# Node row and tile in one bf16 number: a placement product with 105 moving columns, and expert ids made last

## The chip, the cores and the metric

The kernel runs on one core of one Trainium2 chip. The metric is device time in microseconds (us), from the start of the program to its end. The engines named below are PE (TensorE matmul; its weight loads, PEld, are shown apart), DVE (VectorE), ACT (ScalarE), POOL (GpSimd) and SP (SyncE, which only issues DMAs here).

## What is computed

A graph layer for 6250 nodes with 256 features: a normalised graph convolution over 100,000 edges, a linear attention over all nodes, and a mixture of experts in which each node picks two of eight experts. The change touches only the step between the router and the experts:

```
logits = einsum('bsd,de->bse', xn, Wr) + br
top_vals, top_idx = top_k(logits, 2)
w = softmax(top_vals)
for e in range(8):
    h = gelu(xn @ W1[e] + b1[e])
    y = y + (h @ W2[e] + b2[e]) * w_full[..., e]
```

The kernel computes each expert only for the nodes that chose it. The 2 x 6250 choices are sorted by expert into 105 tiles of 128 slots, each tile of one expert. For each slot the kernel must know which node to gather and to which row of `results` its output is written.

## The kernel before

The program is a row of phases, each closed by a barrier over all engines (`over(phase)`). Two phases matter here: the router phase (about 834 to 1057 us) and the expert phase behind it (1058 to 1456 us).

**The place products.** At the end of the router phase, DVE knows for each of the 98 columns of choices (49 node tiles, two choices each) and each of the 128 rows the position of that choice in the sorted order, split into a tile number (`hi16`, 0 to 104) and a slot in the tile (`lo16`, 0 to 127). To invert this map the kernel uses PE. For each column c, `lo1` is the one-hot of the slot (128 x 128, the stationary operand) and `hv1` holds the one-hot of the tile times a value (the moving operand); the product adds that value at [slot, tile] of the PSUM bank `psI`. `hv1` has two halves of 105 columns: one with the one-hot times 2*row+1 (made by ACT, `own_rows`, L1498), one with the one-hot times the node's tile number (made by DVE, L1739). So 210 columns move in each of the 98 matmuls (L1458). bf16 holds a row value or a tile number exactly, but not their sum, which is why there are two halves.

The 98 columns go in `NROUND` = 7 rounds of `OHC` = 14. In a round DVE makes `hi1` (L1735), `lo1` (L1737) and the product `hv1` (L1739) for 14 columns in one instruction each; the 14 columns lie innermost in memory, so PE reads both operands with a step of 28 bytes from element to element. `hi1`, `lo1` and `hv1` are double buffered: DVE begins round r+2 when PE has ended round r (`pl_free`).

**Expert ids.** After round 0 DVE computes the expert of each of the 105 tiles (L1745 to L1749) and signals `eid_ok`. SP waits for it, between two parts of its list of stores, and loads the first two tiles' W1 (L1374, L1375).

**The normalised rows.** ACT makes 49 tiles of normalised rows (`norm`, L1495); SP stores them four tiles at a time in the DRAM array `table` (L1365, L1368), through a ring of four buffers (`keep`), from which the expert phase gathers. ACT does 34 of them, then the exponential of the router's softmax (L1510), then in each round two halves of `own_rows` and one `norm`, then the last eight.

**The end.** When the product is closed (L1461, a product with zeros), DVE reads `psI` and works out in eight instructions (L1756 to L1764) the gather index `gat` and the scatter index `sct` of every slot; slots without a node get a row behind the 12,500 real ones (`dump`). Then comes the barrier. In the expert phase POOL gathers rows (L1901), PE transposes them (L1813), multiplies with W1 (L1823) and W2 (L1833), and POOL scatters the result.

Of the kernel before, what the change touches and what calls it, by code (L numbers as in the profile page):

```python
# [4 lines left out]
f32, i32, bf16, f16 = mybir.dt.float32, mybir.dt.int32, mybir.dt.bfloat16, mybir.dt.float16  # L5
ALU, ACT, AX = mybir.AluOpType, mybir.ActivationFunctionType, mybir.AxisListType
P = 128

N, E, D = 6250, 100000, 256
NX, HID, EPS = 8, 512, 1e-5  # L10
# [3 lines left out]
T = -(-N // P)  # L14
# [37 lines left out]
def build(nc, a_x, a_src, a_dst, a_gw, a_cb, a_lnw, a_lnb, a_pre, a_wqkv, a_mk, a_mv, a_wout, a_bout,  # L52
# [5 lines left out]
    with ExitStack() as ctx:  # L58
# [1205 lines left out]
        def lanes(k):  # L1264
# [15 lines left out]
        held_i = rt[:, 1120:1120 + NTILE].bitcast(i32)  # L1280
# [7 lines left out]
        own_i, own = ints[:, 540:542], flat[:, 542:544]  # L1288
        tcol_i, tcol = ints[:, 550:550 + 2 * T], flat[:, 650:650 + T].bitcast(bf16)
# [7 lines left out]
        hv1 = [R2[:, 9408 + 1470 * k:9408 + 1470 * (k + 1)].bitcast(bf16).rearrange("p (j c) -> p j c", c=OHC)  # L1297
               for k in range(2)]
        w1r = RG[:, :].rearrange("p (s f) -> p s f", s=4)
# [9 lines left out]
        with nc.Block() as block:  # L1309
# [35 lines left out]
            pl_own = semaphore(phase, "r_place_rows")  # L1345
# [8 lines left out]
            @block.sync  # L1354
            def _(sp):
                sp.wait_ge(px_ok, T)
                sp.dma_start(R3[:, 0:room], a_w2).then_inc(w2_in, 16)
                sp.wait_ge(x_ok, T)
                sp.dma_start(b2s.rearrange("p e f -> p (e f)"), a_b2.unsqueeze(0).to_broadcast([P, NX * D])).then_inc(b2_in, 16)

                def keep_rows(h):
                    lo, n = 4 * h, min(4, T - 4 * h)
                    sp.wait_ge(n_ok, lo + n)
                    if lo + n < T:
                        sp.dma_start(table[lo * P:(lo + n) * P, :].rearrange("(t p) f -> p t f", p=P),  # L1365
                                     n_rows[:, 4 * (h % NR):4 * (h % NR) + n, :]).then_inc(keep[h % NR], 16)
                    else:
                        sp.dma_start(table[lo * P:N, :], n_rows[0:TAIL, 4 * (h % NR), :]).then_inc(keep[h % NR], 16)  # L1368

                for h in range(NB4 - 4):  # L1370
                    keep_rows(h)
                sp.wait_ge(eid_ok, 1)
                for t in range(2):
                    e = nc.sync.value_load(eid_i[0:1, t:t + 1], min_val=0, max_val=NX - 1)  # L1374
                    sp.dma_start(w1r[:, t, :], a_w1[bass.ds(e, 1), :, :].rearrange("a p f -> (a p) f")).then_inc(w_in[t], 16)  # L1375
                for h in range(NB4 - 4, NB4):
                    keep_rows(h)
                sp.wait_ge(w2_in, 16)
                for k in range(NR):
                    sp.wait_ge(keep[k], 16 * ((NB4 - k + NR - 1) // NR))  # L1380

            @block.tensor
            def _(pe):
# [69 lines left out]
                nc.tensor.matmul(psI[:, 0:2 * NTILE], zero16[:, 0:P], zero16[:, 0:2 * NTILE], start=True, stop=False)  # L1453
# [7 lines left out]
                nc.tensor.matmul(psI[:, 0:2 * NTILE], zero16[:, 0:P], zero16[:, 0:2 * NTILE], start=False,  # L1461
# [3 lines left out]
            def _(act):  # L1465
# [32 lines left out]
                def own_rows(r, k):  # L1498
                    if k == 0:
                        act.wait_ge(pl_hot, r + 1)  # L1500
                        if r >= 2:
                            act.wait_ge(pl_free, r - 1)
                    act.activation(hv1[r % 2][:, 0:NTILE, k:OHC:2], hi1[r % 2][:, :, k:OHC:2], ACT.Copy,
                                   scale=own[:, k:k + 1]).then_inc(pl_own, 1)

                early = 34
# [4 lines left out]
                act.wait_ge(ready, 3)  # L1511
                for r in range(NROUND):
                    for k in range(2):
                        own_rows(r, k)
                    norm(early + r)
                for t in range(early + NROUND, T):
                    norm(t)

            @block.gpsimd
            def _(pool):  # L1520
# [3 lines left out]
                nc.gpsimd.iota(own_i, pattern=[[1, 2]], base=1, channel_multiplier=2).then_inc(pl, 1)  # L1524
                nc.gpsimd.iota(dump_i, pattern=[[P, NTILE]], base=2 * N + 1, channel_multiplier=1).then_inc(pl, 1)
                nc.gpsimd.iota(tcol_i, pattern=[[1, T], [0, 2]], base=0, channel_multiplier=0).then_inc(pl, 1)
                pool.wait_ge(pl, 3)
                nc.gpsimd.tensor_copy(dump, dump_i).then_inc(pl, 1)
                nc.gpsimd.tensor_copy(own, own_i).then_inc(ready, 1)
                nc.gpsimd.tensor_copy(tcol, tcol_i).then_inc(ready, 1)  # L1530
# [10 lines left out]
            def _(v):  # L1541
# [188 lines left out]
                def place(r):  # L1730
                    if r >= 2:
# [7 lines left out]
                    nc.vector.tensor_tensor(hv1[r % 2][:, NTILE:2 * NTILE, :], hi1[r % 2],  # L1739
                                            tcol[:, here].unsqueeze(1).to_broadcast(wide), ALU.mult).then_inc(pl_tile, 1)  # L1740

                for r in range(NROUND):
                    place(r)
                    if r == 0:
                        ch.done(nc.vector.tensor_tensor(past, iwin[0:1, 0:NSTEP].unsqueeze(2).to_broadcast([1, NSTEP, NX - 1]),  # L1745
                                                        cumt[0:1, 0:NX - 1].unsqueeze(1)
                                                        .to_broadcast([1, NSTEP, NX - 1]), ALU.is_ge))
                        ch.done(nc.vector.tensor_reduce(eidf, past, AX.X, ALU.add))
                        nc.vector.tensor_copy(eid_i, eidf).then_inc(eid_ok, 1)  # L1749
# [266 lines left out]
```

## Time and profile before

| | us |
|---|---|
| median of 3 runs | 1534.99 (1532.45 to 1539.14) |
| profiled execution, its own time | 1534.88 |
| span of its instructions | 1532.9 |
| PE busy / weight load busy | 1266.2 / 1107.0 |
| DVE / ACT / POOL busy | 960.1 / 450.8 / 764.0 |
| mean granted TensorE clock | 0.934 |

Times in the trace count from the span's start. The page's L418 line is the same kind of product in the first phase, where the in-degrees are counted: 14 columns a round, both operands with the same 28-byte step, the stationary one 128 wide, the moving one 49. A timeline row gives the start, the length from first start to last end of a run of like instructions, the engine, the line, the operation and its count, and in brackets how long the engine had been idle and what ended that. The granted clock is a share of 2.4 GHz, so 0.50 is 1.2 GHz. A matmul's duration reaches from its start to the end that the profiler models, so back-to-back matmuls overlap; the distance of their starts tells the rate.

### The profile page before, as it was taken

To read this page: it belongs to the slowest core of one execution; us is meant where nothing else is said; L and a number is where in the kernel's file an instruction comes from. 1 tells how busy PE (TensorE), PEld (TensorE's weight loads), DVE (VectorE), ACT (ScalarE), POOL (GpSimd) and SP (SyncE) were. 2 spreads that over 40 slices of the span, in tenths; PEclk is the share of its full clock that TensorE was granted. 3 is DMA by queue.
4 is the path that set the end of the run, shared out by engine and by line. 5 is a ranking of instruction groups with operands and counts; after the bars stand their busy time and mean duration, and the time that the engine had idled before them with its cause. 6 is when DMAs were issued, how large, how long until landed. Compare 5 with 4: busy or idle time off the path is not lost. (4 is left out here: it accounts for less than half of the span.)

```text
span 1532.9 us, 30179 instructions
## 1 busy us (share of the span) xinstructions
PE 1266.2 (83%) x8310; PEld 1107.0 (72%) x8311; DVE 960.1 (63%) x2700; ACT 450.8 (29%) x1322; POOL 764.0 (50%) x822
## 2 busy tenths in 40 slices
PE   1797678888888999998987978767999999999910
PEld 1685477887787889887775856523999999999900
DVE  3998777777688888778854977863222223222347
ACT  1565600122123333333221023463322332233200
POOL 2001577777777777777774023201555555555400
PEclk9999898999999999999998989955999999999965
DMA  6002533333466667778895000252666666666658
GB/s 204 15 0 69 168 106 105 104 105 106 126 177 174 199 196 215 211 219 261 279 283 166 1 1 1 108 181 94 211 210 209 216 209 210 212 215 207 192 198 314
DMA packets 142678, 248.24 MB, mean 162 GB/s; under 512 B 22826, under 2 KB 99108, under 8 KB 142324
## 3 DMA queue, kind: packets, MB, share of 16 engines
q1 hardware_dynamic: 99256, 146.13, 29.8%
q0 software_dynamic: 34320, 93.76, 21.0%
q10 hardware_dynamic: 9004, 7.21, 1.4%
q8 instruction: 41, 0.67, 0.2%
q14 instruction: 57, 0.47, 0.1%
HBM read 213.65 MB, written 33.36 MB: 161 GB/s over the span
## 5 line engine op out<-in xcount | busy, mean ns | idle before, releaser
L716 POOL DMA_INDIRECT RG<-table,srci x504 | 496.0, 984 | 157.7 <-issue 154.4
L733 PE MATMUL ps<-S_t,RG 128*128 128x96 f32 x2016 | 283.7, 278 | 51.7 <-DMA RG<-table,srci 47.8
L733 PEld LDWEIGHTS ps<-S_t,RG 128*128 128x128 f32 x2016 | 270.3, 195 | 74.8 <-DMA RG<-table,srci 60.8
L1881 DVE TENSOR_TENSOR R<-ps,R 128x256 f32<-128x256 f32 x105 | 44.6, 425 | 278.4 <-PE ps L1833 278.4
L1823 PE MATMUL ps<-R,RG 128*128 128x128 f32 x1680 | 207.2, 277 | 0.0
L987 DVE TENSOR_TENSOR R<-R,ps 128x392 f32 x280 | 157.0, 561 | 79.3 <-PE ps L743 59.7
L755 PE MATMUL ps<-zrow,R 128*128 128x256 f32 x686 | 193.3, 386 | 12.8 <-DMA zrow<-table 7.9
L1856 ACT ACTIVATE R<-ps,RG 128x128 f32<-128x128 f32 x420 | 119.7, 368 | 279.0 <-PE ps L1823 279.0
L1833 PE MATMUL ps<-R 128*128 x840 | 198.6, 380 | 0.0
L1823 PEld LDWEIGHTS ps<-R,RG 128*128 128x128 f32 x1680 | 198.4, 194 | 0.0
L1907 POOL DMA_INDIRECT results<-R,S_t x105 | 103.7, 988 | 164.0 <-DVE R L1881 160.8
L1833 PEld LDWEIGHTS ps<-R 128*128 128x128 f32 x840 | 151.8, 191 | 16.1
L1901 POOL DMA_INDIRECT R<-table,S_t x105 | 101.9, 971 | 104.4 <-PEq L1806 71.6
L755 PEld LDWEIGHTS ps<-zrow,R 128*128 128x128 f32 x686 | 121.6, 190 | 33.1 <-DMA zrow<-table 16.4
L859 ACT ACTIVATE R<-iwin 128x256 f32<-128x256 f32 (+2 forms) x127 | 61.4, 490 | 174.1 <-PE ps L755 164.1
L418 PE MATMUL ps<-RG 128*128 128x49 bf16 x784 | 82.4, 276 | 15.1 <-DVE RG L509 15.1
L418 PEld LDWEIGHTS ps<-RG 128*128 128x128 bf16 x784 | 72.6, 144 | 25.0 <-DVE RG L509 21.5
L1534 POOL TENSOR_TENSOR R<-R,slot 128x256 f32<-128x256 f32 x49 | 35.6, 727 | 109.5 <-DVE slot L1618 109.4
L1872 DVE TENSOR_SCALAR R<-ps,gamma,beta 128x128 f32<-128x128 f32 x212 | 76.6, 403 | 11.9 <-PE ps L1813 11.9
L946 DVE TENSOR_TENSOR S_t<-dstrel,iwin 128x384 f32<-128x384 f32 x126 | 69.4, 551 | 0.7
L508 DVE TENSOR_TENSOR RG<-R,RG 128x1792 bf16<-128x1792 bf16 x56 | 61.0, 1090 | 8.4 <-PE ps L418 8.0
L959 DVE TENSOR_TENSOR R<-R,ps 128x192 f32 x126 | 44.4, 353 | 30.9 <-issue 27.9
(352 smaller groups left out, 1883.3 us busy)
## 6 DMA issues: line engine op xcount, KB each, us to landing
RG<-in_w SPq DMA_DIRECT2D x106, 514.0 KB
zrow<-table SPq DMA_DIRECT2D x336, 128.0 KB
R<-results SPq DMA_DIRECT2D x48, 256.0 KB, 12.2
RG<-table,srci POOLq DMA_INDIRECT x504, 3.4
table<-RG SPq DMA_DIRECT2D x12, 512.0 KB, 2.9
table<-R SPq DMA_DIRECT2D x12, 512.0 KB, 3.3
out<-R ACTq DMA_DIRECT2D x48, 128.0 KB, 5.4
R<-in_x SPq DMA_DIRECT2D x6, 896.0 KB
```

What stands on the lines that cost most here:

```text
L418: last = nc.tensor.matmul(ps[7][:, 0:T], ohlo[k][:, :, c], ohhi[k][:, :, c], start=False, stop=False)
L716: nc.gpsimd.indirect_dma_start(out=grows[:, s, :], out_offset=None, in_=table, in_offset=bass.IndirectOffsetOnAxis(ap=srci[:, ND + q, c:c ...
L733: last = nc.tensor.matmul(window(q % 2)[:, h, :], grows[:, s, h * P:(h + 1) * P], S_t[:, q % 2, c, :], start=c == 0, stop=c == GC - 1)
L755: nc.tensor.matmul(psD[:, 0:D], adj[b % 2][0:n, j, :], zrow[0:n, i % ZR, :], start=j == 0, stop=j == T - 1).then_inc(z_used, 1)
L946: nc.vector.tensor_tensor(S_t[:, q % 2, :, :], dstrel[:, ND + q, :].unsqueeze(2).to_broadcast([P, GC, WIN]), iwin[:, 0:WIN].unsqueeze(1).t ...
L987: nc.vector.tensor_tensor(win, win, psK[m % 2][:, 0:T * DW].rearrange("p (j w) -> p j w", w=DW), ALU.add).then_inc(cnt_ok, 1)
L1823: last = nc.tensor.matmul(psH[s % 2][:, h * P:(h + 1) * P], w1r[:, s, k * HID + h * P:k * HID + (h + 1) * P], ur[:, s % 2, k, :], start=k ...
L1833: last = nc.tensor.matmul(psY[s % 2][:, 0:D], hr[:, s % 2, h, :], w2_sb[:, bass.ds(e, 1), h, :].rearrange("p a f -> p (a f)"), start=h == ...
L1856: last = act.activation(hr[:, s % 2, h, :], psH[s % 2][:, h * P:(h + 1) * P], ACT.Gelu, bias=w1r[:, s, KC * HID + h:KC * HID + h + 1])
L1872: last = nc.vector.tensor_scalar(ur[:, s % 2, k, :], psX[s % 2][:, k * P:(k + 1) * P], gamma[:, k:k + 1], beta[:, k:k + 1], ALU.mult, ALU.add)
L1901: nc.gpsimd.indirect_dma_start(out=xr[:, t % 4, :], out_offset=None, in_=table, in_offset=bass.IndirectOffsetOnAxis(ap=gat[:, t:t + 1], ax ...
L1907: nc.gpsimd.indirect_dma_start(out=results, out_offset=bass.IndirectOffsetOnAxis(ap=sct[:, t:t + 1], axis=0), in_=yr[:, t % 4, :], in_offs ...
```

## The change

One bf16 number carries both values. For column j = 2*tile + choice and row p, an int16 is made with the bits 128*(134 + j) + p, and read as bf16: p stands in the seven bits of the significand, 134 + j in the exponent. A one-hot times this number is exact, and a sum with zeros in PSUM too. POOL makes the array `code` at the start of the phase (L1512, L1515 of the changed kernel). `hv1` is now 105 columns wide and made by DVE alone, ACT's `own_rows` and its semaphore are gone, and PE waits for DVE only. After the products DVE takes tile, choice and row out of the bits with shifts and masks: twelve instructions in place of eight.

The expert ids are computed after the last round instead of after round 0, and SP issues all thirteen stores of rows before it waits for them. ACT does 24 rows, the exponential, and then the other 25 rows without a break.

```
-        hv1 = [R2[:, 9408 + 1470 * k:9408 + 1470 * (k + 1)].bitcast(bf16).rearrange("p (j c) -> p j c", c=OHC)
+        hv1 = [R2[:, 9408 + 735 * k:9408 + 735 * (k + 1)].bitcast(bf16).rearrange("p (j c) -> p j c", c=OHC)
                for k in range(2)]
+        CODE0 = 134 * P
...
-                for h in range(NB4 - 4):
+                for h in range(NB4):
                     keep_rows(h)
                 sp.wait_ge(eid_ok, 1)
...
-                for h in range(NB4 - 4, NB4):
-                    keep_rows(h)
...
                     pe.wait_ge(pl_tile, r + 1)
-                    pe.wait_ge(pl_own, 2 * r + 2)
                     for c in range(OHC):
-                        last = nc.tensor.matmul(psI[:, 0:2 * NTILE], lo1[r % 2][:, :, c], hv1[r % 2][:, :, c],
+                        last = nc.tensor.matmul(psI[:, 0:NTILE], lo1[r % 2][:, :, c], hv1[r % 2][:, :, c],
...
-                early = 34
+                early = 24
...
-                act.wait_ge(ready, 3)
-                for r in range(NROUND):
-                    for k in range(2):
-                        own_rows(r, k)
-                    norm(early + r)
-                for t in range(early + NROUND, T):
+                for t in range(early, T):
                     norm(t)
...
+                nc.gpsimd.iota(code_i, pattern=[[P, 2 * T]], base=CODE0, channel_multiplier=1).then_inc(pl, 1)
+                nc.gpsimd.tensor_copy(code16, code_i).then_inc(ready, 1)
...
-                    nc.vector.tensor_tensor(hv1[r % 2][:, NTILE:2 * NTILE, :], hi1[r % 2],
-                                            tcol[:, here].unsqueeze(1).to_broadcast(wide), ALU.mult).then_inc(pl_tile, 1)
+                    nc.vector.tensor_tensor(hv1[r % 2], hi1[r % 2], code[:, here].unsqueeze(1).to_broadcast(wide),
+                                            ALU.mult).then_inc(pl_tile, 1)
...
                 ch.done(nc.vector.tensor_copy(held, psI[:, 0:NTILE]))
-                ch.done(nc.vector.scalar_tensor_tensor(held, psI[:, NTILE:2 * NTILE], float(2 * P), held, ALU.mult,
-                                                       ALU.add))
-                nc.vector.tensor_scalar(pad, held, 0.5, None, ALU.is_lt)
-                ch.done(nc.vector.tensor_scalar(held_i, held, -1.0, 0.0, ALU.add, ALU.max))
-                ch.done(nc.vector.tensor_scalar(gat, held_i, 1, None, ALU.arith_shift_right))
-                ch.done(nc.vector.tensor_tensor(pad, pad, dump, ALU.mult))
-                ch.done(nc.vector.scalar_tensor_tensor(pad, held, -1.0, pad, ALU.add, ALU.add))
-                ch.done(nc.vector.tensor_copy(sct, pad))
+                ch.done(nc.vector.tensor_scalar(code_q, held.bitcast(i32), 16, None, ALU.arith_shift_right))
+                nc.vector.tensor_scalar(tile_q, code_q, 8, None, ALU.arith_shift_right)
+                nc.vector.tensor_scalar(row_q, code_q, P - 1, None, ALU.bitwise_and)
+                ch.done(nc.vector.tensor_scalar(pad, held, 0.5, None, ALU.is_lt))
+                ch.done(nc.vector.tensor_scalar(tokf, tile_q, float(-(CODE0 >> 8)), float(P), ALU.add, ALU.mult))
+                nc.vector.tensor_tensor(pad, pad, dump, ALU.mult)
+                ch.done(nc.vector.tensor_tensor(tokf, tokf, row_q, ALU.add))
+                ch.done(nc.vector.tensor_scalar(gat, tokf, 0.0, None, ALU.max))
+                ch.done(nc.vector.tensor_scalar(code_q, code_q, 7, 1, ALU.arith_shift_right, ALU.bitwise_and))
+                ch.done(nc.vector.scalar_tensor_tensor(pad, gat, 2.0, pad, ALU.mult, ALU.add))
+                ch.done(nc.vector.tensor_tensor(sct, pad, code_q, ALU.add))
```

What stands in a row on DVE, at the first two rounds of the kernel before (L1745, L1748 and L1749 are the expert ids):

```order
L1735 TENSOR_TENSOR R2<-R3,RG 128x1470
L1737 TENSOR_TENSOR R2<-R3,RG 128x1792
L1739 TENSOR_TENSOR R2<-R2,S_t 128x1470
L1745 TENSOR_TENSOR slot<-iwin,R3 1x742
L1748 TENSOR_REDUCE R3<-slot 1x106
L1749 CAST S_t<-R3 1x106
L1735 TENSOR_TENSOR R2<-R3,RG 128x1470
```

And on DVE at the last round of the changed kernel (L1729, L1732 and L1733 are the expert ids there, L1735 to L1737 the softmax weights, L1740 the first read of `psI`):

```order
L1720 TENSOR_TENSOR R2<-R3,RG 128x1470
L1722 TENSOR_TENSOR R2<-R3,RG 128x1792
L1724 TENSOR_TENSOR R2<-R2,S_t 128x1470
L1729 TENSOR_TENSOR slot<-iwin,R3 1x742
L1732 TENSOR_REDUCE R3<-slot 1x106
L1733 CAST S_t<-R3 1x106
L1735 TENSOR_SCALAR x1s<-x1b 128x49
L1736 RECIPROCAL x1s<-x1s 128x49
L1737 TENSOR_TENSOR x1b<-x1b,x1s 128x49
L1740 COPY R3<-ps7 128x105
```

The three instructions of the expert ids moved from between rounds 0 and 1 to behind round 6.

On SP, the same place in the kernel before (`table` is written by the stores, `in_w1` read by the first two weight loads):

```order
L1365 DMA table<-R2 128x4x256 x9
L1374 TENSOR_LOAD S_t
L1374 ISA x2
L1375 ISA
L1375 DMA RG<-in_w1 128x1028
L1374 TENSOR_LOAD S_t
L1374 ISA x2
L1375 ISA
L1375 DMA RG<-in_w1 128x1028
L1365 DMA table<-R2 128x4x256 x3
L1368 DMA table<-R2 106x256
```

And in the changed kernel:

```order
L1368 DMA table<-R2 128x4x256 x12
L1371 DMA table<-R2 106x256
L1377 TENSOR_LOAD S_t
L1377 ISA x2
L1378 ISA
L1378 DMA RG<-in_w1 128x1028
L1377 TENSOR_LOAD S_t
L1377 ISA x2
L1378 ISA
L1378 DMA RG<-in_w1 128x1028
```

The two weight loads moved behind the last four stores.

## Rows read from the trace of the kernel before

**Rows 1.** Windows: us, busy (xcount) of PE PEld DVE ACT POOL, PEclk, DMA, GB/s
```profile
1007.00:1054.70 47.70, 37.89 (x100) 14.02 (x100) 26.52 (x42) 29.64 (x45) 0.00 (x0) 0.50 0.34 112
...
1065.00:1456.00 391.00, 390.44 (x2705) 364.29 (x2706) 112.07 (x312) 118.57 (x416) 199.76 (x204) 0.99 0.67 206
```

**Rows 2.** Timeline of PE, end of the router phase and first expert tiles
```profile
1017.16 37.36 PE L1458 MATMUL ps<-R 128*128 128x210 bf16 x98 [9.75 <-ACT R L1503]
1054.35 0.35 PE L1461 MATMUL ps<-slotb 128*128 128x210 bf16 x1
1063.25 0.69 PE L1813 MATMUL ps<-ident,R 128*128 128x128 f32 x2 [8.55 <-DMA R<-table,S_t]
...
1066.04 3.62 PE L1823 MATMUL ps<-R,RG 128*128 128x128 f32 x16
...
1074.37 1.84 PE L1823 MATMUL ps<-R,RG 128*128 128x128 f32 x15
```

**Rows 3.** Timeline of DVE over rounds 0 to 2
```profile
1012.06 0.93 DVE L1735 TENSOR_TENSOR R<-R,RG 128x1470 bf16<-128x1470 bf16 x1
...
1013.91 0.92 DVE L1739 TENSOR_TENSOR R<-R,S_t 128x1470 bf16<-128x1470 bf16 x1
1014.74 0.91 DVE L1745 TENSOR_TENSOR slot<-iwin,R 1x742 f32<-1x742 f32 x1
...
1016.77 0.91 DVE L1735 TENSOR_TENSOR R<-R,RG 128x1470 bf16<-128x1470 bf16 x1
...
1022.69 0.93 DVE L1735 TENSOR_TENSOR R<-R,RG 128x1470 bf16<-128x1470 bf16 x1 [3.18 <-PE ps L1458]
```

**Rows 4.** Instructions by line: duration ns min/median/max, first and last start
```profile
L1458 PE MATMUL ps<-R x98: 551/559/563, 1017.2 to 1054.0; 128*128 128x210 bf16 x98
...
L418 PEld LDWEIGHTS ps<-RG x784: 138/142/168, 44.3 to 134.5; 128*128 128x128 bf16 x196
...
L421 PE MATMUL ps<-slotb x1: 225/225/225, 134.7 to 134.7; 128*128 128x49 bf16 x1
```

**Rows 5.** Timeline of PE's weight loads, one round of the in-degree product
```profile
55.44 1.30 PEld L418 LDWEIGHTS ps<-RG 128*128 128x128 bf16 x14 [0.16 <-DVE RG L509]
```

**Rows 6.** Timeline of ACT from the second batch of norms on
```profile
1004.56 8.95 ACT L1495 ACTIVATE R<-R,zs_b,zs_s 128x256 f32<-128x256 f32 x18 [4.27 <-DMA table<-R]
1013.53 1.28 ACT L1510 ACT_TABLE_LOAD   x1
...
1014.97 2.05 ACT L1503 ACTIVATE R<-R,S_t 128x735 bf16<-128x735 bf16 x2
```

**Rows 7.** SP: two rows of its timeline, one of its waits (us, times, longest)
```profile
1021.46 1.84 SPq L1375 DMA_DIRECT2D RG<-in_w  x2
...
1051.40 0.33 SPq L1368 DMA_DIRECT2D table<-R  x1
...
SPq L1380 <- DMA table<-R: 4.8, 2, 4.6
```

**Rows 8.** Timeline of DVE from its last round to the end of the phase
```profile
1046.62 0.18 DVE L1751 TENSOR_SCALAR x1s<-x1b 128x49 f32<-128x49 f32 x1
...
1047.34 0.21 DVE L1753 TENSOR_TENSOR x1b<-x1b,x1s 128x49 f32<-128x49 f32 x1
1054.81 0.27 DVE L1756 COPY R<-ps 128x105 f32<-128x105 f32 x1 [7.26 <-PE ps L1461]
...
1055.41 0.22 DVE L1759 TENSOR_SCALAR R<-R 128x105 f32<-128x105 f32 x1
1055.54 0.21 DVE L1760 TENSOR_SCALAR R<-R 128x105 int32<-128x105 f32 x1
1055.79 0.22 DVE L1761 TENSOR_SCALAR S_t<-R 128x105 int32<-128x105 int32 x1
1056.04 0.27 DVE L1762 TENSOR_TENSOR R<-R,S_t 128x105 f32<-128x105 f32 x1
...
1056.65 0.22 DVE L1764 CAST S_t<-R 128x105 int32<-128x105 f32 x1
```

More of the change, by code:

```diff
@@ L5 @@
 f32, i32, bf16, f16 = mybir.dt.float32, mybir.dt.int32, mybir.dt.bfloat16, mybir.dt.float16
+i16 = mybir.dt.int16
 ALU, ACT, AX = mybir.AluOpType, mybir.ActivationFunctionType, mybir.AxisListType
@@ L1279, in build @@
         held = rt[:, 1010:1010 + NTILE]
-        held_i = rt[:, 1120:1120 + NTILE].bitcast(i32)
+        code_q = rt[:, 1120:1120 + NTILE].bitcast(i32)
+        tokf = rt[:, 1240:1240 + NTILE]
+        tile_q, row_q = (rt[:, 610 + 110 * k:610 + 110 * k + NTILE].bitcast(i32) for k in range(2))
         tl_i = rt[:, 1230:1230 + NX].bitcast(i32)
@@ L1287, in build @@
         dump_i = ints[:, 430:430 + NTILE]
-        own_i, own = ints[:, 540:542], flat[:, 542:544]
-        tcol_i, tcol = ints[:, 550:550 + 2 * T], flat[:, 650:650 + T].bitcast(bf16)
+        code_i, code16 = ints[:, 550:550 + 2 * T], flat[:, 650:650 + T].bitcast(i16)
+        code = flat[:, 650:650 + T].bitcast(bf16)
         hi1 = [R2[:, 735 * k:735 * (k + 1)].bitcast(bf16).rearrange("p (j c) -> p j c", c=OHC) for k in range(2)]
@@ L1344, in build @@
             pl_tile = semaphore(phase, "r_place_tiles")
-            pl_own = semaphore(phase, "r_place_rows")
             pl_free = semaphore(phase, "r_place_used")
@@ L1452, in _ @@
                 pe.wait_ge(cum_ok, 1)
-                nc.tensor.matmul(psI[:, 0:2 * NTILE], zero16[:, 0:P], zero16[:, 0:2 * NTILE], start=True, stop=False)
+                nc.tensor.matmul(psI[:, 0:NTILE], zero16[:, 0:P], zero16[:, 0:NTILE], start=True, stop=False)
                 for r in range(NROUND):
                     pe.wait_ge(pl_tile, r + 1)
-                    pe.wait_ge(pl_own, 2 * r + 2)
                     for c in range(OHC):
-                        last = nc.tensor.matmul(psI[:, 0:2 * NTILE], lo1[r % 2][:, :, c], hv1[r % 2][:, :, c],
+                        last = nc.tensor.matmul(psI[:, 0:NTILE], lo1[r % 2][:, :, c], hv1[r % 2][:, :, c],
                                                 start=False, stop=False)
                     last.then_inc(pl_free, 1)
-                nc.tensor.matmul(psI[:, 0:2 * NTILE], zero16[:, 0:P], zero16[:, 0:2 * NTILE], start=False,
+                nc.tensor.matmul(psI[:, 0:NTILE], zero16[:, 0:P], zero16[:, 0:NTILE], start=False,
                                  stop=True).then_inc(inv_ok, 1)
@@ L1496, in norm @@
                                    bias=zs_b[:, t:t + 1]).then_inc(n_ok, 1)
[L1498 to L1504, printed above, removed]
-                early = 34
+                early = 24
                 for t in range(early):
@@ L1523, in _ @@
                                allow_small_or_imprecise_dtypes=True).then_inc(ready, 1)
[L1524 to L1530, printed above, removed]
+                nc.gpsimd.iota(dump_i, pattern=[[P, NTILE]], base=2 * N, channel_multiplier=1).then_inc(pl, 1)
+                nc.gpsimd.iota(code_i, pattern=[[P, 2 * T]], base=CODE0, channel_multiplier=1).then_inc(pl, 1)
+                pool.wait_ge(pl, 2)
+                nc.gpsimd.tensor_copy(dump, dump_i).then_inc(ready, 1)
+                nc.gpsimd.tensor_copy(code16, code_i).then_inc(ready, 1)
                 def residual(t):
@@ L1738, in place @@
                     v.wait_ge(pl_hot, r + 1)
-                    nc.vector.tensor_tensor(hv1[r % 2][:, NTILE:2 * NTILE, :], hi1[r % 2],
-                                            tcol[:, here].unsqueeze(1).to_broadcast(wide), ALU.mult).then_inc(pl_tile, 1)
+                    nc.vector.tensor_tensor(hv1[r % 2], hi1[r % 2], code[:, here].unsqueeze(1).to_broadcast(wide),
+                                            ALU.mult).then_inc(pl_tile, 1)
                 for r in range(NROUND):
                     place(r)
[L1744 to L1749, printed above, removed]
+                ch.done(nc.vector.tensor_tensor(past, iwin[0:1, 0:NSTEP].unsqueeze(2).to_broadcast([1, NSTEP, NX - 1]),
+                                                cumt[0:1, 0:NX - 1].unsqueeze(1)
+                                                .to_broadcast([1, NSTEP, NX - 1]), ALU.is_ge))
+                ch.done(nc.vector.tensor_reduce(eidf, past, AX.X, ALU.add))
+                nc.vector.tensor_copy(eid_i, eidf).then_inc(eid_ok, 1)
                 v.wait_ge(ex_ok, 1)
```

## The prediction

> **What bounds the kernel now.** I read the stretches first, then the timelines of PE, DVE, ACT and SP over the 50 us before the expert phase. The expert phase is one stretch in which PE is busy 390.44 of 391 us at a granted clock of 0.99 [rows 1]; its length doesn't depend on when it starts, so whatever the router phase gives up moves the end of the program by the same amount. In the router phase the place product decides. From 1017.16 to 1054.70 PE does 98 matmuls without a pause [rows 2]; DVE, which feeds them, stands still for 3.18 us before round 2 until PE frees a buffer [rows 3], and for 7.26 us at the end until PE closes the product [rows 8]. After that come DVE's eight index instructions, to 1056.87, and 6.38 us of barrier, gather and first transpose, to 1063.25 [rows 2, 8]. SP's last store, issued by 1051.73, had landed after a wait of 4.6 us, at about 1056.3 [rows 7], so DVE closes the phase, with SP only 0.6 us ahead. The clock is 0.50 through the product, that is 1.2 GHz [rows 1].
>
> **PE's start.** The product starts at 1017.16, released by ACT [rows 2]. ACT was late: 34 norms, a table load and the exponential kept it until 1015, then it needed 2.05 us for the two halves of round 0 [rows 6]. DVE's own part of round 0 ended at 1013.91 + 0.92 = 1014.83 [rows 3]. With ACT out of it PE starts a semaphore later, 0.06 us: 1014.89, which is 2.27 us earlier.
>
> **PE's rate, the term that carries the sum.** The 98 matmuls take 37.36 us, of which the last one's own duration is 0.559 [rows 2, 4]: (37.36 - 0.559)/97 = 0.379 us from start to start, or 1.807 ns for each of 210 moving columns. The trace has no product with 105 such columns, but it has one with 49, same weight shape and same step in memory, L418. Fourteen of its weight loads take 1.30 us including the last one's 0.142 [rows 4, 5]: (1.30 - 0.142)/13 = 0.0891 us, or 1.818 ns a column. Both are proportional to the columns with nothing left for a fixed part, if both ran at the same clock. The profile gives 1.00 for that early stretch, but the closing matmul L421 with 49 packed columns took 0.225 us, and L1461 with 210 at 0.50 took 0.35 [rows 2, 4]: 0.125 to 0.13 us for 161 columns is 0.79 ns each, about one cycle at 1.2 GHz. A matmul at 2.4 GHz would not lie on that line. I take it that L418 ran at 1.2 GHz too and that the 1.00 stands only for "no change recorded yet". Then 105 columns take 105 x 1.807 = 0.190 us, and a round of 14 takes 2.66 us in place of 5.31. The upper bound, if L418 did run at full clock, comes from adding the 128 weight columns to the moving ones: 0.379 x 233/338 = 0.261 us, 3.66 us a round. I take 0.190, since it needs no coincidence.
>
> The rule of the Trainium skill that speaks of this (TensorE: Matmul & The Clock Gate, "Back-to-back issue gap") gives one cycle a column, 87.5 ns for 105 at 1.2 GHz, with 107 ns for the weights. The trace disagrees: 379 ns for 210 where the rule gives 175. By the rule the sum would be that of rival B below. The Trainium skill (SBUF — State Buffer), in the note on 16-byte cachelines under its port table, also says that reads whose step crosses such a line pay a penalty, and the step here is 28 bytes; the trace agrees.
>
> **DVE and PE together.** DVE's three instructions of a round keep it 2.68 us when nothing holds it (1012.06 to 1014.74) and are complete after 2.77 [rows 3]. Round r+2 needs the buffer of round r. After PE starts round r, DVE may begin r+2 after 13 x 0.190 + 0.37 + 0.05 = 2.89 us (0.37 is the duration 0.559 less 105 columns; 0.05 is 1022.69 less the end of PE's round 0). Then 2.77 to build and 0.06 to start PE: 5.72 us for two rounds, while PE itself needs 5.32 and DVE 5.36. So neither engine alone is the bound, but the hand-over through two buffers. PE starts rounds 0, 2, 4, 6 at 1014.89, 1020.61, 1026.33, 1032.05. The closing matmul starts at 1032.05 + 2.66 = 1034.71. DVE read PSUM 0.46 us after that point before [rows 2, 8]; with 0.09 less for 105 packed columns it reads at 1035.08. Before it was 1054.81: **19.73 us earlier**.
>
> **Expert ids made last.** They took 2.03 us after round 0 (1014.74 to 1016.77) [rows 3]. That was hidden, since DVE then waited 3.18. Now they stand behind round 6: DVE begins that round at 1026.33 + 2.89 = 1029.22, is free at 1031.90, has the ids at 1033.93 and the softmax weights 0.97 later (1046.62 to 1047.55 and the step on) [rows 8], at 1034.90. PE's last round covers it, with 0.18 us to spare. Cost 0; if PE were faster it would show, up to 3.0 us.
>
> **SP.** Its waiting instruction is now the one for the ids, with nothing behind it but the two weight loads; all stores are issued before. It issues the loads about 0.8 and 2.3 us after 1033.93 (two took 1.84 us from first to last [rows 7]), done at 1036.6. The phase ends for DVE at 1037.9, so it isn't held. The loads are needed when the first hidden product starts, 2.79 us behind the first transpose (1066.04 - 1063.25) [rows 2], now about 1047: 10 us later. The second load may still be moving when the first gather is; I allow 0 to 1 us, take 0.
>
> **ACT and the stores.** ACT waited 4.27 us for the ring after 16 norms and did 18 more in 8.95 us [rows 6], 0.50 each. Now it does 8, the exponential (1.5 us) and 25: 1004.56 + 4.0 + 1.5 + 12.5 = 1022.6. Stores follow and land by about 1027 even with the 4.6 us of the last one. That is 10 us before anyone needs them; cost 0. The removed `own_rows` were ACT's, the removed POOL instructions stood at the start of the phase ahead of nothing that waits.
>
> **The index instructions.** Before: 1054.81 to 1056.87, 2.06 us. Steps read there [rows 8]: an instruction that the next waits for costs its duration and 0.03 to 0.04, so 0.25 for a TENSOR_SCALAR and 0.30 for a copy from PSUM or a two-operand one; one without a wait costs 0.13 (1055.41 to 1055.54), a two-operand one then about 0.18. Now: one copy 0.30, five waited scalar steps (L1741, L1744, L1745, L1748, L1749) 1.25, two unwaited 0.26, one unwaited two-operand 0.18, two waited two-operand 0.60, the last 0.27: 2.86 us. **0.80 us more.** Shifts and masks on integers cost the same as others (L1761).
>
> **Sum.** -19.73 + 0.80 = -18.9 us. Against the profiled execution's 1534.88: 1516.0. That execution lies 0.1 us from the median of the runs, 1534.99, so the forecast is **1516.0 us**.
>
> **Rivals.**
> (A) PE's rate isn't proportional: 0.261 us a matmul. Then PE is the bound, seven rounds of 3.66 us from 1014.89, the closing matmul at 1040.5, DVE reads at 1040.9: 13.9 us earlier, less 0.8. 1521.8 us. For it speaks the 1.00 shown at L418; against it L421's duration.
> (B) PE is faster than I take it and DVE alone sets the pace: round 6 begins at 1014.74 + 5 x 2.68 = 1028.14, is done 2.68 later, and ids and softmax weights, 3.0 us, lie bare: read at 1033.8, 21.0 us earlier, less 0.8. 1514.7 us. It would also follow if the granted clock rose in the product. Against both stands a matmul stream that took 379 ns a matmul and stayed at 0.50 for 37 us [rows 1, 2]. The Trainium skill's one cycle a column (TensorE: Matmul & The Clock Gate, "Back-to-back issue gap") would give this case.
> (C) The change doesn't do what it says: the stream is bound by the strided weights, which stay 128 wide, at 0.379 us. Only the earlier start stays: 2.27 + 0.09 less 0.8. 1533.3 us. Against it: L418 loads the same weights every 0.089 us [rows 5].
> (D) Slower: the clock. PE enters the expert phase at 0.50 after a gap of 8.55 us, and 16 matmuls of L1823 take 3.62 us where later 15 take 1.84 [rows 2]. A tile costs 1.66 us more there, and the W2 half, with as many column passes, the same: 3.3 us. Before, the clock was full within three tiles. If the shorter product left PE at the low clock for more tiles, six of them eat the gain, and eight more make 1542 us. Against it: after 37 us of matmuls the clock was still 0.50, so the product bought nothing there, and the gap stays the same.
>
> **How the numbers follow.** Forecast, within 3 us of 1516: 0.66. Rival B 0.08, A 0.13, C 0.05, D 0.03. The rest, 0.05, is my sum with something between 3 and 6 us laid bare (the weight loads against the first gathers, a late store). All but C and D are faster by more than 0.5% (7.7 us, about what a measurement of this kernel can tell from no change): faster 0.91; same 0.06 (C and part of the rest); slower 0.03. The range takes in B with a little scatter of the runs and A: 1512 to 1522.5; it leaves out C, D and the end of the rest.
>
> **What would show it.** In the changed kernel: 98 matmuls of 128x105 in about 20 us, 0.190 from start to start, at 0.50; DVE starting rounds 2 to 6 on PE's release, with waits of a few tenths only; ids made under the last round; ACT idle after about 1023; two W1 loads issued at about 1035; the first read of `psI` at 1035.1 and the phase's last DVE instruction near 1037.9; the first gather 1.9 us later; the expert phase as long as before, its first two tiles at the low clock. Wrong would be: a distance of 0.26 or 0.38 between matmuls, PE waiting for the first W1, or a clock that stays at 0.50 past the third tile.

## The result and the profile after

The changed kernel took 1520.33 us, median of four runs (1520.58, 1520.08, 1514.08 and one run of 4200.72, for which the record shows no cause and which is left out of the comparison), against 1534.84 for the kernel before, also of four. The ratio of the others is 0.9891, 95% interval 0.9869 to 0.9913, so the kernel is faster by 0.9 to 1.3%, between 13 and 20 us. Forecast were 1516.0 us and a range of 1512 to 1522.5. The profiled execution took 1520.58 us (span 1518.8), 14.3 us less than the profiled one before.

The timeline of PE over the same place as [rows 2] (L1458 is the place product, L1461 closes it, L1800 is the first transpose of the expert phase, L1810 the W1 product; a row gives start, length, count and the idle time before):

```profile
1019.74 17.13 PE L1458 MATMUL ps<-R 128*128 128x105 bf16 x84 [7.55 <-DVE R L1724]
1037.02 2.90 PE L1458 MATMUL ps<-R 128*128 128x105 bf16 x14 [0.16 <-DVE R L1724]
1039.74 0.27 PE L1461 MATMUL ps<-slotb 128*128 128x105 bf16 x1
1049.22 0.69 PE L1800 MATMUL ps<-ident,R 128*128 128x128 f32 x2 [9.21 <-DMA R<-table,S_t]
...
1051.84 3.62 PE L1810 MATMUL ps<-R,RG 128*128 128x128 f32 x16
```

The product that took 37.36 us now takes 20.2. In its last round 14 matmuls take 2.90 us, of which 0.37 are the last one's own duration, so they start 0.195 us apart (forecast 0.190). The product is released by DVE (L1724, the multiplication that makes `hv1`), not by ACT. DVE over the same rounds as [rows 3] and up to the reading of `psI` as in [rows 8]:

```profile
1016.92 0.92 DVE L1720 TENSOR_TENSOR R<-R,RG 128x1470 bf16<-128x1470 bf16 x1
...
1018.76 0.92 DVE L1724 TENSOR_TENSOR R<-R,S_t 128x1470 bf16<-128x1470 bf16 x1
1019.60 0.92 DVE L1720 TENSOR_TENSOR R<-R,RG 128x1470 bf16<-128x1470 bf16 x1
...
1022.69 0.93 DVE L1720 TENSOR_TENSOR R<-R,RG 128x1470 bf16<-128x1470 bf16 x1 [0.34 <-PE ps L1458]
...
1028.44 0.93 DVE L1720 TENSOR_TENSOR R<-R,RG 128x1470 bf16<-128x1470 bf16 x1 [0.28 <-PE ps L1458]
...
1034.20 0.93 DVE L1720 TENSOR_TENSOR R<-R,RG 128x1470 bf16<-128x1470 bf16 x1 [0.29 <-PE ps L1458]
...
1036.88 0.91 DVE L1729 TENSOR_TENSOR slot<-iwin,R 1x742 f32<-1x742 f32 x1
...
1039.61 0.21 DVE L1737 TENSOR_TENSOR x1b<-x1b,x1s 128x49 f32<-128x49 f32 x1
1040.11 0.27 DVE L1740 COPY R<-ps 128x105 f32<-128x105 f32 x1 [0.30 <-PE ps L1461]
...
1042.70 0.27 DVE L1751 TENSOR_TENSOR S_t<-R 128x105 int32<-128x105 f32 x1
```

DVE's waits in the product have shrunk from 3.18 to about 0.3 us, one in every second round: that is the hand-over through two buffers. The expert ids (from L1729) and softmax weights (to L1737) lie under PE's last round, with 0.30 us to spare. ACT and SP, as in [rows 6] and [rows 7]:

```profile
1014.83 12.40 ACT L1495 ACTIVATE R<-R,zs_b,zs_s 128x256 f32<-128x256 f32 x25
...
1027.25 0.33 SPq L1371 DMA_DIRECT2D table<-R  x1
1039.92 1.52 SPq L1378 DMA_DIRECT2D RG<-in_w  x2
```

ACT is done at 1027.2 and the last store is issued by 1027.6, 15 us before DVE ends the phase; the two weight loads are issued by 1041.4, 1.5 us before DVE ends the phase.

All these times lie 4.86 us later than they should beside the kernel before: round 0 begins at 1016.92 in place of 1012.06, although little ahead of it was changed: instructions of POOL that nobody waits for, a narrower product with zeros that opens `psI`, and, in the last 4 us, the order of ACT's work. This offset is what separates 1520.6 from the forecast. Counted from round 0:

| from the start of round 0, us | before | after | difference | forecast |
|---|---|---|---|---|
| PE's first product | 5.10 | 2.82 | -2.28 | -2.27 |
| DVE reads `psI` | 42.75 | 23.19 | -19.56 | -19.73 |
| last index instruction ends | 44.81 | 26.05 | -18.76 | -18.93 |
| first W1 product | 53.98 | 34.92 | -19.06 | -18.9 |
| end of the span | 520.84 | 501.88 | -18.96 | -18.9 |

### The profile page after: what moved, and what is told of

Read it like the earlier page. It is cut to its first block and busy times, and to the rows that moved or that the text cites. A ratio compares the mean times of both kernels' runs of the same rounds, so it can differ in the third digit from the quotient of the medians.

```text
span 1518.8 us, 30154 instructions
## 1 busy us (share of the span) xinstructions
PE 1258.1 (83%) x8310; PEld 1113.7 (73%) x8311; DVE 959.7 (63%) x2704; ACT 436.9 (29%) x1308; POOL 760.0 (50%) x820
## 5 line engine op out<-in xcount | busy, mean ns | idle before, releaser
L734 PEld LDWEIGHTS ps<-S_t,RG 128*128 128x128 f32 x2016 | 276.3, 198 | 70.7 <-DMA RG<-table,srci 57.2
L734 PE MATMUL ps<-S_t,RG 128*128 128x96 f32 x2016 | 289.6, 282 | 46.4 <-DMA RG<-table,srci 43.6
L756 PE MATMUL ps<-zrow,R 128*128 128x256 f32 x686 | 197.0, 393 | 13.1 <-DMA zrow<-table 9.2
L1810 PE MATMUL ps<-R,RG 128*128 128x128 f32 x1680 | 206.8, 277 | 0.0
L1810 PEld LDWEIGHTS ps<-R,RG 128*128 128x128 f32 x1680 | 198.0, 194 | 0.0
L960 DVE TENSOR_TENSOR R<-R,ps 128x192 f32 x126 | 44.3, 352 | 33.6 <-issue 27.7
```

The source lines that it names most:

```text
L734: last = nc.tensor.matmul(window(q % 2)[:, h, :], grows[:, s, h * P:(h + 1) * P], S_t[:, q % 2, c, :], start=c == 0, stop=c == GC - 1)
L756: nc.tensor.matmul(psD[:, 0:D], adj[b % 2][0:n, j, :], zrow[0:n, i % ZR, :], start=j == 0, stop=j == T - 1).then_inc(z_used, 1)
L1810: last = nc.tensor.matmul(psH[s % 2][:, h * P:(h + 1) * P], w1r[:, s, k * HID + h * P:k * HID + (h + 1) * P], ur[:, s % 2, k, :], start=k ...
```

## Experiments

The experiments ran on three chips on which the kernel before takes longer, with 1667.21 and 1673.37 us (medians) and 1673.82 us (one run): the phase over the edges, from 176 us to the router phase, lasts 796 us in the second profile of the kernel before, in place of 660. The stretch from the router phase's first instruction to the end of the program is the same to 0.02 us in the two profiles of the kernel before, and to 0.1 us in the two of the changed one. So single stretches are compared from the start of round 0, and whole times within one chip: the changed kernel again, width alone, expert ids early and three buffers ran on the first; the kernel before again, ids late and the packed operand on the second; the probe and all operands packed on the third. The kernel before again, the probe and the two packed kernels ran once each, so from these only stretches of the trace are read.

**The same kernels again.** Is the 4.86 us ahead of round 0 scatter, or does the change cost something there?

> The changed kernel, unaltered, for more runs and a second profile. From the start of DVE's round 0 to its first read of psI 23.2 us as in the first profile of it (42.75 before), from there to the first transpose of the expert phase 9.1 us. My theory: the stretch from round 0 to the program's end is 18.9 us shorter than before in every profile, and what the first profile showed ahead of it (round 0 began 4.86 us later than in the profile of before) is scatter of the edge phase, so the start of round 0 will lie elsewhere in this profile, 1012 to 1017, and the ratio near 0.9877. Rival: the change makes the phases ahead of it slower by about 3 us, then round 0 begins at 1016 to 1017 again and the ratio stays at 0.989 to 0.990.

> The kernel before, unaltered, for a second profile. If the start of round 0 scatters from execution to execution, it lies elsewhere than at 1012.06 here, by up to 5 us; if the changed kernel is slower ahead of it for a reason of its own, it lies at 1012 again. From round 0 to the read of psI 42.75 us either way.

The kernel before, unaltered:

```profile
1147.96 0.93 DVE L1735 TENSOR_TENSOR R<-R,RG 128x1470 bf16<-128x1470 bf16 x1
...
1190.50 0.27 DVE L1756 COPY R<-ps 128x105 f32<-128x105 f32 x1 [7.27 <-PE ps L1461]
```

The changed kernel, unaltered:

```profile
1147.86 0.92 DVE L1720 TENSOR_TENSOR R<-R,RG 128x1470 bf16<-128x1470 bf16 x1
...
1171.08 0.27 DVE L1740 COPY R<-ps 128x105 f32<-128x105 f32 x1 [0.30 <-PE ps L1461]
```

Round 0 begins at 1147.96 in the one and 1147.86 in the other, on two chips: no offset. In four profiles of the changed kernel and its variants on the first chip, which ahead of round 0 differ at most in the width of a product with zeros, it begins at 1147.86, 1146.42, 1142.39 and 1150.49. So that start scatters by 8 us, more than the 4.86. From round 0 to the end of the span the kernel before took 520.84 us both times, the changed one 501.88 and 502.04: 18.96 and 18.80 us less. The ratio of the changed kernel's six runs on the first chip is 0.9878 (0.9857 to 0.9899), -20 us. From round 0 to the read of `psI` it was 42.54 us in the kernel before (42.75 the first time) and 23.22 in the changed one (23.19).

The traces of the first pair also tell where the 4.86 us arise. POOL's first instruction of the router phase, in the kernel before and in the changed one:

```profile
835.88 0.40 POOL L1521 COPY RG<-beta 128x256 f32<-128x256 f32 x1 [14.46 <-POOLq L69]
```

```profile
839.27 0.40 POOL L1508 COPY RG<-beta 128x256 f32<-128x256 f32 x1 [21.16 <-POOLq L70]
```

So 3.39 us are there when the router phase begins, and 1.47 are added in it before round 0. That stretch takes 176.2 us in both profiles of the kernel before and 176.9 to 177.7 in those of the changed kernel and its variants, which looks like a small cost of the change; but it takes 177.39 in the run with the ids late, whose instructions ahead of round 0 are those of the kernel before. It is made right at the start: the phase's first 16 matmuls (L1388 before) take 5.40 and 5.13 us in the two profiles of the kernel before, 6.19 in the run with the ids late, and 5.84 to 6.43 in the others, and over the first 6 us the granted clock is 0.72 in the first profile of the kernel before and 0.55 in that of the changed one. So the clock rises later or earlier there, which is scatter too. The expectations named 1012 to 1017 for round 0, a figure of the first chip; only its other half, "elsewhere", can be said to have held.

**Width alone.** The changed kernel with every column moved twice (the products with zeros that open and close `psI` are widened too):

```
-                        last = nc.tensor.matmul(psI[:, 0:NTILE], lo1[r % 2][:, :, c], hv1[r % 2][:, :, c],
+                        last = nc.tensor.matmul(psI[:, 0:2 * NTILE].rearrange("p (k j) -> p k j", k=2), lo1[r % 2][:, :, c],
+                                                hv1[r % 2][:, :, c].unsqueeze(1).to_broadcast([P, 2, NTILE]),
```

> The changed kernel, but each of the 98 matmuls moves the 105 columns twice (210 columns, the second half into columns of psI that nobody reads). Nothing else is altered. If PE's rate goes by columns: 0.379 us a matmul, PE the bound again; from DVE's round 0 to the read of psI 2.83 + 98 x 0.379 + 0.46 = 40.4 us, 17.3 us more than the changed kernel and about 1.5 us less than before in all. Rival, that ACT's part in making hv1 was what held PE before: 0.2 to 0.3 us a matmul here, the read at 25 to 32 us.

PE's timeline in it:

```profile
1149.24 37.45 PE L1458 MATMUL ps<-R 128*128 128x210 bf16 x98 [7.47 <-DVE R L1725]
1186.51 0.36 PE L1462 MATMUL ps<-slotb 128*128 128x210 bf16 x1
```

98 matmuls in 37.45 us, 0.380 each, as before the change, though ACT has no part in it. `psI` is read 40.55 us after round 0 begins (forecast 40.4), 17.4 later than in the changed kernel; the ratio to the kernel before is 0.9992 (0.9977 to 1.0007), no difference that the runs can show. So of the 19.6 us that the product gives, 17.4 are the columns and about 2.2 are ACT's exit. The longer index chain then costs 0.8 of the whole.

**What a moving column costs.** Two runs. In the first `hv1` is stored so that PE reads it packed:

```
-        hv1 = [R2[:, 9408 + 735 * k:9408 + 735 * (k + 1)].bitcast(bf16).rearrange("p (j c) -> p j c", c=OHC)
+        hv1 = [R2[:, 9408 + 735 * k:9408 + 735 * (k + 1)].bitcast(bf16).rearrange("p (c j) -> p j c", c=OHC)
```

> The changed kernel with hv1 stored column by column, so that PE reads the moving operand packed and DVE writes it with a step of 210 bytes. The weights keep their 28-byte step. If the step of the moving operand makes 1.8 ns a column: within a round 0.09 to 0.11 us a matmul in place of 0.19, PE waiting for DVE between rounds; DVE's multiplication gets slower than 0.92 us (1.6 us, one element a cycle), so the read of psI lies at 24 to 27 us. Rival, that the weights' step or a fixed time per matmul makes it: 0.19 us stays.

One multiplication on DVE and one round on PE:

```profile
1154.05 6.60 DVE L1724 TENSOR_TENSOR R<-R,S_t 128x1470 bf16<-128x1470 bf16 x1
```

```profile
1168.89 1.45 PE L1458 MATMUL ps<-R 128*128 128x105 bf16 x14 [6.74 <-DVE R L1724]
```

With the last one's 0.294 us taken off, 14 matmuls in 1.45 us are 0.089 each, 105 columns at a cycle of 1.2 GHz. The granted clock is 0.50 there too. The step of the moving operand it is. DVE pays far more than I expected for writing with a step of 210 bytes: 6.60 us for 1470 elements, 4.5 ns each, seven times the 0.92 and four times the 1.6 expected, and `psI` is read only after 60.3 us (expected 24 to 27).

But 0.089 is also what the early product L418 showed with 49 columns [rows 5], on which my rate rested. Was that 49 strided columns or the 128 strided weights? The probe adds bursts of zeros ahead of the closing matmul:

```
+                for c in range(OHC):
+                    nc.tensor.matmul(psI[:, 0:16], lo1[0][:, :, c], zero16[:, 0:16], start=False, stop=False)
+                for c in range(OHC):
+                    nc.tensor.matmul(psI[:, 0:NTILE], lo1[0][:, :, c], zero16[:, 0:NTILE], start=False, stop=False)
+                for c in range(OHC):
+                    nc.tensor.matmul(psI[:, 0:16], zero16[:, 0:P], hv1[0][:, 0:16, c], start=False, stop=False)
+                for c in range(OHC):
+                    nc.tensor.matmul(psI[:, 0:49], zero16[:, 0:P], hv1[0][:, 0:49, c], start=False, stop=False)
+                for c in range(OHC):
+                    nc.tensor.matmul(psI[:, 0:NTILE], zero16[:, 0:P], hv1[0][:, :, c], start=False, stop=False)
```

> The changed kernel with five bursts of 14 matmuls ahead of the closing one, all of which add zeros to psI: one-hot weights with the 28-byte step and 16 packed columns of zeros; the same weights and 105 packed columns; packed zero weights and 16, 49 and 105 columns of hv1 with the 28-byte step. It asks what the 0.089 us of the early product with 49 columns was. By my prediction's reading, 1.8 ns for each moving column and weights that are hidden: 105 strided columns 0.190 us, 49 strided ones 0.088, 105 packed ones 0.0875 (as in the run with the packed operand, where 14 took 1.45 us, 0.089 each), and 16 packed columns with strided weights clearly less, 0.06 or below. Rival: loading 128 strided weights takes 0.089 us and was the bound in the early product, then 16 packed columns with strided weights also take 0.089, and that the early product lay on the line through 210 columns was chance.

PE's timeline, one row per burst:

```profile
1174.93 0.95 PE L1462 MATMUL ps<-slotb,R 128*128 128x16 bf16 x14
1175.74 1.43 PE L1464 MATMUL ps<-slotb,R 128*128 128x105 bf16 x14
1176.97 0.64 PE L1466 MATMUL ps<-R,slotb 128*128 128x16 bf16 x14
1177.45 1.43 PE L1468 MATMUL ps<-R,slotb 128*128 128x49 bf16 x14
1178.70 2.83 PE L1470 MATMUL ps<-R,slotb 128*128 128x105 bf16 x14
```

And how long one of them lasts (minimum, median, maximum in ns):

```profile
L1462 PE MATMUL ps<-slotb,R x14: 186/204/205, 1174.9 to 1175.7; 128*128 128x16 bf16 x14
...
L1464 PE MATMUL ps<-slotb,R x14: 282/292/295, 1175.7 to 1176.9; 128*128 128x105 bf16 x14
...
L1466 PE MATMUL ps<-R,slotb x14: 190/196/220, 1177.0 to 1177.4; 128*128 128x16 bf16 x14
...
L1468 PE MATMUL ps<-R,slotb x14: 254/270/273, 1177.4 to 1178.6; 128*128 128x49 bf16 x14
...
L1470 PE MATMUL ps<-R,slotb x14: 368/369/370, 1178.7 to 1181.2; 128*128 128x105 bf16 x14
```

With one duration taken off and the rest divided by 13: strided weights with 16 packed columns 0.057 us, and with 105 packed columns 0.0875; packed weights with 16 strided columns 0.034, with 49 strided columns 0.089 and with 105 strided columns 0.189. The four for which the expectation has a figure came as it says. Strided weights put a floor of 0.057 us under a matmul, which 105 packed columns hide; 49 strided columns alone, with packed weights, make the 0.089. So L418 was bound by its moving columns and had, by its pace, the same 1.2 GHz as here, and the line from 49 over 105 to 210 columns is real: 1.82, 1.80 and 1.81 ns a column. In the product of the changed kernel the 105 columns take 0.195 us, 1.85 ns each. The burst differs from it in its packed weights and in a DVE that makes no operands meanwhile; no run separates the two.

**Expert ids early.** The changed kernel with the ids behind round 0 again, and SP's loads between the stores:

```
                 for r in range(NROUND):
                     place(r)
+                    if r == 0:
+                        ch.done(nc.vector.tensor_tensor(past, iwin[0:1, 0:NSTEP].unsqueeze(2).to_broadcast([1, NSTEP, NX - 1]),
...
+                        nc.vector.tensor_copy(eid_i, eidf).then_inc(eid_ok, 1)
```

> The changed kernel with the expert ids back behind round 0 and SP's two weight loads back between the stores. My theory: DVE no longer waits 3 us there, so the 2.03 us now delay round 1 and through the two buffers later rounds; the read of psI 24.8 us after round 0 begins, 1.6 us later than in the changed kernel; the time 1.6 us more. Rival, that the late weight loads cost something at the start of the expert phase: the time is the same or less, and the stretch from DVE's last index instruction to the first W1 product (8.9 us in the changed kernel's profile) gets shorter by 1 us or more.

DVE's end of the product in it:

```profile
1163.14 0.92 DVE L1726 TENSOR_TENSOR R<-R,S_t 128x1470 bf16<-128x1470 bf16 x1
1163.98 0.18 DVE L1738 TENSOR_SCALAR x1s<-x1b 128x49 f32<-128x49 f32 x1
...
1167.22 0.27 DVE L1743 COPY R<-ps 128x105 f32<-128x105 f32 x1 [2.32 <-PE ps L1463]
```

`psI` is read 24.83 us after round 0 begins (1142.39), as expected, 1.6 later than in the changed kernel, and DVE has 2.32 us of idle time there, which is where the changed kernel puts the ids. The first W1 product comes no sooner for it: from the last index instruction to it are 8.55 us here, 8.87 and 8.30 in the two profiles of the changed kernel. So the late weight loads cost nothing to be seen. Over the whole program 0.9914 (0.9894 to 0.9934) against 0.9878 points the same way, but by 6 us where the trace has 1.6, and the intervals overlap.

**Expert ids late, in the kernel before:**

> The kernel before (210 columns, ACT making half of hv1) with only the second part of the change: expert ids behind round 6, SP's stores all ahead of the weight loads. My theory: no difference (0 +- 0.5 us from round 0 to the expert phase), since the ids were hidden in DVE's wait for PE and are hidden at the end too. Rival, that a good part of the gain comes from freeing DVE after round 0: 2 us less.

Ratio 1.0006 (0.9988 to 1.0023); `psI` read after 42.73 us. The part alone does nothing for the product. The trace shows one small cost that I had not expected, in SP's last store, its two weight loads and its wait behind them:

```profile
1190.45 0.33 SPq L1368 DMA_DIRECT2D table<-R  x1
1192.40 2.60 SPq L1375 DMA_DIRECT2D RG<-in_w  x2
...
SPq L1378 <- DMA table<-R: 1.5, 1, 1.5
```

In this kernel ACT still finishes its norms late. SP's last store goes out at 1190.45, 39.3 us after round 0 begins, as in the two profiles of the kernel before (39.3 and 39.1). But the weight loads behind it are issued until 1195.0, and after them SP still waited 1.5 us for a store to land, so until about 1196.5, 45.4 us after round 0; in the kernel before that was at 44.3. DVE ends at 1195.91, and the first gather comes at 1198.45, 2.54 us later in place of 1.87. I read this as the loads delaying the store and SP closing the phase in DVE's place, 0.6 us behind it; no run isolates it, and the whole times don't show it. In the changed kernel the stores are out 12 us ahead of the loads, and SP has no such wait: there the loads may stand last.

**Three buffers.** Does the hand-over set the round?

```
...
-                    if r >= 2:
-                        v.wait_ge(pl_free, r - 1)
+                    if r >= 3:
+                        v.wait_ge(pl_free, r - 2)
...
```

> The changed kernel with three buffers for lo1 and hv1 in place of two, DVE beginning round r+3 when PE has ended round r. If the hand-over through two buffers sets the 2.87 us a round: DVE then never waits between rounds, 2.68 us a round, the read of psI at 21.9 us after round 0 begins, 1.3 us earlier, with the expert ids and softmax weights just hidden. Rival, that PE alone is the bound: no change, DVE waits 0.2 us a round still.

DVE had no wait between rounds any more, and one at the end:

```profile
1168.36 0.92 DVE L1724 TENSOR_TENSOR R<-R,S_t 128x1470 bf16<-128x1470 bf16 x1
...
1172.69 0.27 DVE L1740 COPY R<-ps 128x105 f32<-128x105 f32 x1 [0.56 <-PE ps L1461]
```

`psI` is read 22.20 us after round 0 begins (1150.49), 1.0 us earlier than in the changed kernel; 1.3 were expected. PE ran through its 98 matmuls without a pause:

```profile
1153.31 19.18 PE L1458 MATMUL ps<-R 128*128 128x105 bf16 x98 [7.56 <-DVE R L1724]
```

That is 0.194 us each, 2.71 a round against DVE's 2.67: with the hand-over out of the way PE is the bound by a few hundredths, where the prediction had DVE ahead (2.66 and 2.68). It is the better kernel by that microsecond in the stretch; the runs can't show it (0.9898, 0.9878 to 0.9918, against 0.9878 for the changed kernel on the same chip).

**All operands packed.** The last idea for a faster product stores `hi1`, `lo1`, `hv1` and the iota column by column, so that DVE writes packed too:

> The changed kernel with hi1, lo1, hv1 and the iota all stored column by column, so that PE reads both operands packed and DVE writes packed; DVE's broadcast operand (a number per row and column) then repeats along the innermost dimension instead of an outer one. PE: 0.09 us a matmul or a little less. DVE: if its pace of 0.92 us for 1470 elements needs a packed innermost dimension on every operand, it falls to about one element a cycle, 1.6 and 1.9 us, some 4.9 us a round, and psI is read at about 36 us after round 0 begins. Rival: DVE keeps 2.68 us a round, the read lies at 21.5 us and this would be the better kernel.

```profile
1157.33 1.69 DVE L1720 TENSOR_TENSOR R<-R,RG 128x1470 bf16<-128x1470 bf16 x1
1158.93 2.02 DVE L1722 TENSOR_TENSOR R<-R,RG 128x1792 bf16<-128x1792 bf16 x1
1160.87 1.68 DVE L1724 TENSOR_TENSOR R<-R,S_t 128x1470 bf16<-128x1470 bf16 x1
```

```profile
1162.61 1.42 PE L1458 MATMUL ps<-R 128*128 128x105 bf16 x14 [10.02 <-DVE R L1724]
```

PE's 14 matmuls take 1.42 us, 0.087 each, as expected. But DVE's instructions take 1.69 and 2.02 us in place of 0.92 and 1.08, 5.14 us a round, with the broadcast operand repeating in the innermost dimension, and the expert ids and softmax weights lie bare behind its last round; `psI` is read after 38.9 us (expected 36). What the layout with a 28-byte step costs PE, it more than gives back on DVE.

## Why the prediction was right

**PE's start.** Right: 2.28 us earlier, forecast 2.27, by DVE's release.

**PE's rate, proportional to the columns at 1.8 ns.** Right, with 0.195 us a matmul measured against 0.190, and it was the term that could have gone wrong. The reading that carried it, L418 at 1.2 GHz in spite of the 1.00 shown there, was an inference from one matmul's duration [rows 4]. The probe has now measured it: 49 strided columns take 0.089 us at 0.50. The coincidence that I set aside was nearer than I thought, since strided weights have a floor of their own, at 0.057 us; by an estimate from that and 1.8 ns a column, an early product with fewer than 32 columns would have shown that floor and no slope. The 107 ns for the weights that the prediction quotes under "Back-to-back issue gap" stand in another section of that page of the Trainium skill (TensorE: Matmul & The Clock Gate, "LDWEIGHTS (loading the stationary operand)"); the probe disagrees with them, as strided weights were loaded every 57 ns. Rivals A (0.261 us) and C (weights as the bound, 0.379) fall by the 0.195 us of the changed kernel itself.

**Two buffers.** Right in kind, 0.03 to 0.04 us short in size for two rounds: DVE begins rounds 2, 4 and 6 at distances of 5.75 and 5.76 us, forecast 5.72. Run with three buffers, the waits between the rounds are gone. Rival B, DVE's pace alone, would have read at 21.7 us; 23.19 was measured. The 0.17 us that the sum missed at the read of `psI` (23.19 from round 0 against 23.02) are 0.12 in the three pairs of rounds and 0.06 in the last round, for the most part the 0.195 in place of 0.190.

**Expert ids at no cost.** Right, with 0.30 us to spare against the 0.18 forecast. Left early they would cost 1.6 us, which the prediction didn't say: it treated the move as harmless, and it is worth a twelfth of the gain.

**SP, ACT and the stores.** Right as to the changed kernel. In the kernel before SP was only 0.6 us ahead of DVE at the end, as the prediction says; the run with the ids late suggests that the moved loads alone would have used that up.

**Index chain.** 2.86 us from 1040.11 to 1042.97, forecast 2.86. Costing each instruction by its like, with or without a wait behind it, was exact.

**Rival D, the clock.** It fell: the third tile's W1 product starts 7.95 and 8.10 us after the first in the changed kernel's profiles, 8.33 and 8.34 in those of before.

**The sum.** -18.9 us forecast, -18.96 and -18.80 measured from round 0 on in the two pairs. The whole time came 4.3 us above the forecast in the first measurement, outside the 3 us to which the main case was given 0.66. That isn't a term of the sum but the start of round 0, which the forecast took from one profile of before as if it were fixed. That the range held it was luck: its upper end came from rival A, which did not happen. The scatter of the phases ahead of round 0, up to 8 us, should have been in the range by itself.

What stays open: why round 0 begins up to 8 us apart on one chip after the same work, and why the edge phase takes 136 us more on the chips of the experiments. No run was made for either. The traces show where the 136 us lie: POOL's 504 gathers of that phase (L716) take as long, 496.0 and 493.4 us in the two profiles of the kernel before, but POOL's idle time ahead of them grew from 157.7 to 285.8 us, and 106.8 us of it ended with an event that the profile only calls remote.

## What to carry to other kernels

When two engines feed each other, read what one product costs per moving column from its own start-to-start distances and from another product with the same memory step, and check by a burst of matmuls by themselves that both ran at one clock; the width then tells the gain. Take the hand-over between two buffers as a chain of its own: it can be longer than either engine's work. And when an engine is freed, look at what stands in its idle time: an instruction chain that was free in a long wait has to move to the next one.

## What the runs showed of the hardware

- Moving bf16 columns read with a step of 28 bytes cost 1.8 ns each at a granted clock of 0.50, packed ones 0.83 (105 in 0.0875 us). Weights with that step were loaded every 0.057 us ahead of 16 packed columns; packed weights every 0.034 us ahead of 16 strided ones. The Trainium skill (SBUF — State Buffer, the note on 16-byte cachelines) says that such steps pay a penalty; here it is a factor of 2.2.
- A DVE multiplication of 1470 bf16 elements took 0.92 us with every operand's innermost dimension running through memory, 1.68 with the broadcast operand repeating in the innermost dimension, and 6.60 when it wrote with a step of 210 bytes.
- The profile's granted clock of 1.00 ahead of the first recorded change can't be relied on: the product L418 ran there at the pace that 49 strided columns have at 0.50 (0.089 us), and L421, with 49 packed columns, lasted 0.225 us, on the line of L1461 at 0.50. No run has a strided bf16 product at the full clock to set beside them.
- In the product the granted clock stayed at 0.50 for 20 us in the changed kernel and for 37 us in the one before, with PE at work nearly all the time; in the expert phase's fp32 products it was at 1.00 from the third tile on.
